# Splitting fp32 operands for one-pass matmuls: ScalarE's copy in place of a mask on VectorE

## The reference, cut to what matters

```
# 1  linear attention, 16 heads of 8
q = elu(x @ Wq + bq) + 1 ;  k = elu(x @ Wk + bk) + 1 ;  k = k / sqrt(sum_head(k*k) + 1e-6)
a = (q @ (k^T @ v) per head) @ Wo + bo
x = layernorm(x + (layernorm(x + a) * gamma + beta))
# 2  cross attention over 64 context rows, 16 heads of 64
p = softmax((x @ Wq2) @ (ctx @ Wk2)^T / 8) ;  x = layernorm(x + (p @ (ctx @ Wv2)) @ Wo2)
# 3  gated MLP, 352 wide; inputs and weights rounded in blocks of 16 to a 4-bit grid times max/6
x = layernorm(x + quant(silu(quant(x) @ quant(Wg)^T) * (quant(x) @ quant(Wu)^T)) @ quant(Wd)^T)
```

## Time and profile before

| | |
|---|---|
| median of 3 runs | 372.44 us (372.42 to 372.96) |
| span of the profiled execution | 371.1 us |
| PE busy | 349.7 us (94%) |
| DVE busy | 308.7 us (83%) |
| POOL busy | 269.0 us (73%) |
| ACT busy | 253.6 us (68%) |
| DMA queues | a few per cent of the span each |

### The profile page before, as it was taken

The page is one execution under the profiler, slowest core; times in us unless marked ns, Lnnn a source line. Parts: engine busy times, 40 slices in busy tenths (PEclk is TensorE's granted clock), DMA queues, the critical chain, the costliest instruction groups (busy, mean ns, idle before and its releaser), DMA issues.

```text
span 371.1 us, 7329 instructions
## 1 busy us (share of the span) xinstructions
PE 349.7 (94%) x2147; PEld 267.9 (72%) x2147; DVE 308.7 (83%) x858; ACT 253.6 (68%) x533; POOL 269.0 (73%) x453
## 2 busy tenths in 40 slices
PE   8999989999998999999999999999999999998774
PEld 7788646675775868787678877786767787887653
DVE  3998557567689998869989779979998998999994
ACT  2957766577676677678688767878767666864553
POOL 4404459958988699969689895898988569784535
PEclk9999999999999999999999999999999999999999
DMA  8900100001000001000000000100000000000010
GB/s 248 305 2 16 30 1 16 14 16 29 15 17 14 17 0 44 28 18 16 29 14 17 14 1 17 31 0 0 17 15 2 15 2 1 15 16 14 3 30 28
DMA packets 13586, 10.44 MB, mean 28 GB/s; under 512 B 971, under 2 KB 12396, under 8 KB 13548
## 3 DMA queue, kind: packets, MB, share of 16 engines
q1 hardware_dynamic: 12540, 7.89, 7.1%
q10 hardware_dynamic: 1008, 2.10, 1.7%
HBM read 7.88 MB, written 2.10 MB: 27 GB/s over the span
## 4 chain that ended last, share of the span: by engine, by line
PE 70%; DVE 9%; POOL 8%; issue 6%; ACT 4%; DMA 1%; SPq 0%; POOLq 0%; DVEq 0%
PE A L2892 13%; PE S L2862 12%; PE TP L2852 7%; PE F L2916 6%; PE TP L2880 6%; PE A L2936 5%; PE S L2871 3%; PE A L2813 2%; PE TP L2791 2%; POOL pe L440 2%; PE F L2791 2%; PE S L2791 2%; PE TP L2925 2%; PE A L2826 2%; PE A L2821 1%
## 5 line engine op out<-in xcount | busy, mean ns | idle before, releaser
L440 POOL TENSOR_TENSOR pe<-pe,srec 128x1024 f32<-128x1024 f32 x32 | 60.9, 1904 | 9.2 <-DVE srec L1860 8.9
L2862 PE MATMUL S<-M,x1T 128*128 128x512 f32 x128 | 60.7, 597 | 1.5 <-ACT pe L1076 1.4
L2892 PEld LDWEIGHTS A<-wvoT,wqkT 128*128 128x128 f32 x480 | 56.4, 192 | 3.1 <-issue 1.8
L2892 PE MATMUL A<-wvoT,wqkT 128*128 128x128 f32 x480 | 58.0, 276 | 0.1
L434 POOL TENSOR_TENSOR fold<-pe 128x512 f32<-128x512 f32 x32 | 40.9, 1277 | 14.6 <-ACT pe L1076 14.4
L1843 DVE TENSOR_REDUCE smax<-S 128x16 fp32r<-128x1024 f32 x32 | 38.7, 1211 | 3.3 <-PE S L2862 3.1
L1076 ACT ACTIVATE pe<-S 128x1024 f32<-128x1024 f32 x32 | 32.6, 1019 | 10.6 <-PE S L2871 10.3
L1081 ACT ACTIVATE wqkT<-TP 128x1024 f32<-128x1024 f32 x32 | 32.6, 1018 | 4.3 <-PE TP L2880 4.1
L2862 PEld LDWEIGHTS S<-M,x1T 128*128 128x128 f32 x128 | 22.2, 190 | 18.3 <-issue 15.3
L2916 PE MATMUL F<-w_gu_r,GT 128*128 128x352 f32 x168 | 35.1, 344 | 0.1
L2880 PE MATMUL TP<-ident,pe 128*128 128x128 f32 x256 | 33.5, 274 | 1.6 <-POOL pe L440 0.9
(11 more groups left out here) (247 smaller groups left out, 888.2 us busy)
## 6 DMA issues: line engine op xcount, KB each, us to landing
xT<-in_x_t SPq DMA_DIRECT2D x16, 128.0 KB, 2.2
x_sb<-in_x SPq DMA_DIRECT2D x16, 128.0 KB, 2.2
out<-yf SPq DMA_DIRECT2D x15, 128.0 KB, 1.8
M<-in_fw SPq DMA_DIRECT2D x1, 560.0 KB, 11.0
wqkT<-in_wq_t ACTq DMA_DIRECT2D x2, 256.0 KB, 4.6
wqkT<-in_wk_t ACTq DMA_DIRECT2D x2, 256.0 KB, 6.1
ctx_f<-in_ctx_t ACTq DMA_DIRECT2D x2, 256.0 KB, 7.0
wvoT<-in_wv_t ACTq DMA_DIRECT2D x1, 512.0 KB, 9.4
```

The source lines that it names most:

```text
L440: ge.tensor_tensor(w, w, spread(srec[n % NFO][:, :], HX, R), ALU.mult).then_inc(pn_made, 1)
L2862: last = te.matmul(S[:, half * BANK:half * BANK + BANK], x1T[b % 2][:, t * P:t * P + P], M[:, b // BH, HC * half:HC * half + HC, b % BH * ...
L2892: last = te.matmul(part(A2, t), pT[n % 2][:, j, :], vo[b % 2][:, j, :], start=(j == 0 and b not in SUM_ON_PE), stop=(j == NJ - 1))
```

## The change

The mask goes. ACT copies the source itself into the high half, which is typed fp32r. The low part then subtracts what was written there, read back as fp32. The scratch tile `xf_cut`, the semaphores of the masks and 23 DVE instructions fall away: 2 masks of ctx, 4 of G, 2 of the gate and up weights and 15 of the MLP inputs, one for each of batches 0 to 14. None is added. All that is left stays in its order on every engine; only the operands and the waits of the copies and the subtractions differ.

```diff
@@ POOL
             def context_low(half):
-                pool.wait_ge(c_cut, half + 1)
+                pool.wait_ge(c_high, half + 1)
                 cols = slice(512 * half, 512 * half + 512)
-                ge.tensor_tensor(ctx_r[:, 1, cols], ctx_f[:, cols], high_bits[half], ALU.subtract).then_inc(c_low, 1)
+                ge.tensor_tensor(ctx_r[:, 1, cols], ctx_f[:, cols], ctx_r[:, 0, cols].bitcast(FP32),
+                                 ALU.subtract).then_inc(c_low, 1)
             def gate_up_low(m):
-                pool.wait_ge(gu_cut_made, m + 1)
-                ge.tensor_tensor(w_gu_r[:, 1, m, :], w_gu[:, m, :], gu_cut[m], ALU.subtract).then_inc(gu_low_made, 1)
+                pool.wait_ge(gu_high_made, m + 1)
+                ge.tensor_tensor(w_gu_r[:, 1, m, :], w_gu[:, m, :], w_gu_r[:, 0, m, :].bitcast(FP32),
+                                 ALU.subtract).then_inc(gu_low_made, 1)
@@ ACT
             def context_high(half):
-                act.wait_ge(c_cut, half + 1)
-                sc.activation(ctx_r[:, 0, 512 * half:512 * half + 512], high_bits[half], ACT.Copy).then_inc(c_high, 1)
+                act.wait_ge(ctx_loaded[half], 16)
+                cols = slice(512 * half, 512 * half + 512)
+                sc.activation(ctx_r[:, 0, cols], ctx_f[:, cols], ACT.Copy).then_inc(c_high, 1)
             def g_keep_high(half, par):
-                k = 2 * half + par
-                act.wait_ge(g_cut, k + 1)
-                sc.activation(g_tile(half, par)[0], high_bits[2 + k].rearrange("p (a b) -> p a b", a=4),
+                act.wait_ge(g_made, half + 1)
+                sc.activation(g_tile(half, par)[0], G_BANKS[half][par].rearrange("p (a b) -> p a b", a=4),
                               ACT.Copy).then_inc(g_high, 1)
             def gate_up_high(m):
-                act.wait_ge(gu_cut_made, m + 1)
-                sc.activation(w_gu_r[:, 0, m, :], gu_cut[m], ACT.Copy).then_inc(gu_high_made, 1)
+                act.wait_ge(fwT_kept, m + 1)
+                sc.activation(w_gu_r[:, 0, m, :], w_gu[:, m, :], ACT.Copy).then_inc(gu_high_made, 1)
@@ ACT, keep_xfT(b)
-                    act.wait_ge(xf_cut_made, b + 1)
-                    sc.activation(xf_r[b % 2][:, 0, :], xf_cut[:, :], ACT.Copy).then_inc(xfT_kept, 1)
+                    act.wait_ge(xfT_made, b + 1)
+                    sc.activation(xf_r[b % 2][:, 0, :], A2[:, 0:T * P], ACT.Copy).then_inc(xfT_kept, 1)
@@ DVE
-            def context_cut(half):
...
-            def g_cut_high(half, par):
...
             def g_keep_low(half, par):
                 k = 2 * half + par
-                dve.wait_ge(g_cut, k + 1)
+                dve.wait_ge(g_high, k + 1)
                 ve.tensor_tensor(g_tile(half, par)[1], G_BANKS[half][par].rearrange("p (a b) -> p a b", a=4),
-                                 high_bits[2 + k].rearrange("p (a b) -> p a b", a=4), ALU.subtract).then_inc(g_low, 1)
+                                 g_tile(half, par)[0].bitcast(FP32), ALU.subtract).then_inc(g_low, 1)
-            def gate_up_cut(m):
...
-            def xf_cut_high(b):
-                dve.wait_ge(xfT_made, b + 1)
-                wait_free(dve, xfT_kept, b)
-                ve.tensor_scalar(xf_cut[:, :].bitcast(INT32), A2[:, 0:T * P].bitcast(INT32), HIGH_MASK, None,
-                                 ALU.bitwise_and).then_inc(xf_cut_made, 1)
-
             def xf_keep_low(b):
-                dve.wait_ge(xf_cut_made, b + 1)
-                ve.tensor_tensor(xf_r[b % 2][:, 1, :], A2[:, 0:T * P], xf_cut[:, :], ALU.subtract).then_inc(xf_low_made, 1)
+                dve.wait_ge(xfT_kept, b + 1)
+                ve.tensor_tensor(xf_r[b % 2][:, 1, :], A2[:, 0:T * P], xf_r[b % 2][:, 0, :].bitcast(FP32),
+                                 ALU.subtract).then_inc(xf_low_made, 1)
@@ DVE, the list of steps
             biases()
-            context_cut(0)
-            g_cut_high(0, 0)
-            g_cut_high(0, 1)
             g_keep_low(0, 0)
             k_features(0)
             g_keep_low(0, 1)
             k_sums(0)
-            g_cut_high(1, 0)
-            g_cut_high(1, 1)
             q_features(0)
             g_keep_low(1, 0)
             g_keep_low(1, 1)
             k_guess(0)
-            context_cut(1)
...
```

More of the change, by code:

```diff
@@ L149, in decoder_layer @@
         xam = several("xam", 2, [P, NX])
-        xf_cut = sb("xf_cut", [P, T * P])
         xf_r = [GT[:, k, 0:2 * T, :].rearrange("p (s t) n -> p s (t n)", s=2) for k in range(2)]
@@ L167, in decoder_layer @@
         fw_m, fw_s, fw_r = (hT[1][:, 0, NWB * k:NWB * k + NWB] for k in range(3))
-        gu_cut = [w[:, 1, 0:I] for w in hT]
-        high_bits = [w[:, 512 * k:512 * k + 512] for w in pe_ for k in range(2)]
         A1, A2, S, TP, F = banks("A1", 1), banks("A2", 1), banks("S", 2), banks("TP", 2), banks("F", 2)
@@ L207, in decoder_layer @@
         bias_made = sem("bias_made")
-        c_cut, c_high, c_low = sem("c_cut"), sem("c_high"), sem("c_low")
-        g_made, g_cut, g_high, g_low = sem("g_made"), sem("g_cut"), sem("g_high"), sem("g_low")
+        c_high, c_low = sem("c_high"), sem("c_low")
+        g_made, g_high, g_low = sem("g_made"), sem("g_high"), sem("g_low")
         m_made = sem("m_made")
@@ L234, in decoder_layer @@
         xfT_made, xfT_kept = sem("xfT_made"), sem("xfT_kept")
-        xf_cut_made, xf_low_made = sem("xf_cut_made"), sem("xf_low_made")
-        gu_cut_made, gu_high_made, gu_low_made = sem("gu_cut_made"), sem("gu_high_made"), sem("gu_low_made")
+        xf_low_made = sem("xf_low_made")
+        gu_high_made, gu_low_made = sem("gu_high_made"), sem("gu_low_made")
         gu_made, th_made, hg_made, h_made = sem("gu_made"), sem("th_made"), sem("hg_made"), sem("h_made")
@@ L1715, in biases @@
                                  ALU.subtract).then_inc(bias_made, 1)
-            def context_cut(half):
-                dve.wait_ge(ctx_loaded[half], 16)
-                ve.tensor_scalar(high_bits[half].bitcast(INT32), ctx_f[:, 512 * half:512 * half + 512].bitcast(INT32),
-                                 HIGH_MASK, None, ALU.bitwise_and).then_inc(c_cut, 1)
-            def g_cut_high(half, par):
-                dve.wait_ge(g_made, half + 1)
-                ve.tensor_scalar(high_bits[2 + 2 * half + par].bitcast(INT32), G_BANKS[half][par].bitcast(INT32),
-                                 HIGH_MASK, None, ALU.bitwise_and).then_inc(g_cut, 1)
             def g_keep_low(half, par):
                 k = 2 * half + par
-                dve.wait_ge(g_cut, k + 1)
+                dve.wait_ge(g_high, k + 1)
                 ve.tensor_tensor(g_tile(half, par)[1], G_BANKS[half][par].rearrange("p (a b) -> p a b", a=4),
-                                 high_bits[2 + k].rearrange("p (a b) -> p a b", a=4), ALU.subtract).then_inc(g_low, 1)
+                                 g_tile(half, par)[0].bitcast(FP32), ALU.subtract).then_inc(g_low, 1)
             def m_keep(half, hd):
@@ L1742, in hw_keep @@
                                TP1.rearrange("p (a b) -> p a b", a=4)).then_inc(hw_kept["dve"], 1)
-            def gate_up_cut(m):
-                dve.wait_ge(fwT_kept, m + 1)
-                ve.tensor_scalar(gu_cut[m].bitcast(INT32), w_gu[:, m, :].bitcast(INT32), HIGH_MASK, None,
-                                 ALU.bitwise_and).then_inc(gu_cut_made, 1)
             def weights_max():
@@ L2073, in _ @@
             m_keep(1, 5)
-            gate_up_cut(0)
             keep_kvT(0)
@@ L2077, in _ @@
             m_keep(1, 7)
-            gate_up_cut(1)
             k_sums(2)
@@ L2201, in _ @@
             statistics("post", 4)
-            xf_cut_high(0)
             aggregate("post", 4)
@@ L2229, in _ @@
             statistics("post", 5)
-            xf_cut_high(1)
             xf_keep_low(1)
@@ L2267, in _ @@
             statistics("attn", 6)
-            xf_cut_high(2)
             k_guess(9)
@@ L2318, in _ @@
             q_features(8)
-            xf_cut_high(3)
             keep_kvT(8)
@@ L2329, in _ @@
             statistics("ffn", 2)
-            xf_cut_high(4)
             xf_keep_low(4)
@@ L2385, in _ @@
             attn_residual(9)
-            xf_cut_high(5)
             statistics("attn", 9)
@@ L2434, in _ @@
             statistics("post", 10)
-            xf_cut_high(6)
             xf_keep_low(6)
@@ L2492, in _ @@
             aggregate("attn", 11)
-            xf_cut_high(7)
             xf_keep_low(7)
@@ L2524, in _ @@
             score_max(11, 0)
-            xf_cut_high(8)
             xf_keep_low(8)
@@ L2572, in _ @@
             score_max(12, 1)
-            xf_cut_high(9)
             xf_keep_low(9)
@@ L2585, in _ @@
             score_max(13, 0)
-            xf_cut_high(10)
             xf_keep_low(10)
@@ L2611, in _ @@
             statistics("cross", 12)
-            xf_cut_high(11)
             keep_kvT(15)
@@ L2665, in _ @@
             statistics("cross", 14)
-            xf_cut_high(12)
             aggregate("cross", 14)
@@ L2676, in _ @@
             gate_times(12, 0)
```

(2 more changed lines are left out.)

## The result

| | before | after |
|---|---|---|
| median of 5 runs | 372.69 us | 379.54 us (379.44 to 379.63) |
| ratio | | 1.0182 (95% interval 1.0171 to 1.0193) |
| span of the profiled execution | 371.1 us | 377.9 us |

The profiled execution of after took 379.63 us as a whole, 1.7 us above its span.

The account below looks back on a forecast made before the run. PE was taken as the bound from about 14 us, so only delays reaching PE count: 371.1 us span + 2.3 at the start + 3.1 in the batches + 1.3 around the span = 377.8 us, range 374.0 to 380.3.

Parts of the forecast that it names:

- What bounds the kernel: From about 14 us PE is the bound; DVE time saved gives nothing by itself, only when PE gets its inputs counts.
- The start: G's split waits for ACT's copies, so PE's solid stretch starts at 16.54 us, not 14.26: +2.3 us, not won back.
- Batches 2, 4, 8 and the tail: Later MLP-input subtractions reach PE: +0.4 us, +1.15, +0.6, and +0.65 in the tail (batches 12 and 13).
- Batches 1, 7, 10, 11: Later MLP-input subtractions: +0.3 us in batch 1, nothing in 7 (hidden), 10 and 11 taken as 0.
- What lies around the span: Time of an execution outside the profiled span, taken as 1.3 us and added to the span.
- Only the start costs: Rival: stalls in the batches die out before PE meets them, 374.7 us; chance 0.27.
- The stalls add up: Rival: all 11 later subtractions in the batches reach PE in full, +6.8 us there, 381.5 us; chance 0.12.
- DVE's relief wins: Rival: dropping masks shortens the start by 1.2 us and the batches behind 240 us by 2.6, 368.6 us; chance 0.07.
- Does less than it says: Rival: ACT writes all bits into the high half, leaving the low half zero; time unchanged at 377.8 us; no chance given.
- A lower clock: Rival: PE's new breaks of 0.6 to 1 us at the start lower TensorE's clock; given nothing of its own.

Follow-up runs that it names:

- experiment 5: Changed kernel with ACT's copies of G moved early at the start and its MLP-input copies moved early in eight batches, no masks: 373.03 us, ratio 1.0004.
- experiment 8: Changed kernel with start masks back; in the batches DVE itself copies A2 into the high half and subtracts, ACT's 15 copies removed: 372.92 us, ratio 1.0000.
- experiment 1: Changed kernel with the masks of the context and G put back at the start, MLP inputs still split by ACT's copy: 377.48 us, ratio 1.0122.
- experiment 3: Changed kernel with only ACT's list at the start reordered, so G's copies come earlier: 377.24 us, ratio 1.0118.
- experiment 4: Changed kernel with ACT's MLP-input copy moved ahead by one or two instructions in eight batches, start left as changed: 375.85 us, ratio 1.0088.
- experiment 6: Changed kernel with the DVE mask put back for batches 4 and 11 alone: 377.79 us, ratio 1.0129.
- experiment 2: Changed kernel with the DVE mask put back for all 15 MLP inputs, start still split by ACT's copy: 376.40 us, ratio 1.0089.

## Why the prediction was right, and where it was short

The forecast was 377.8 us, 5.1 us above the 372.69 of before; measured were 379.54, 6.9 above, inside the range.

**What bounds the kernel: right.** Experiments 5 and 8 take 8 us off DVE or 5 off ACT and change nothing.

**The start: right.** Copies at 9.85, 11.86, 14.71 and 15.2 us, the third product at 16.68; +2.3 was said, +2.4 came. Experiments 1 and 3 give it back in two ways. The saying that it is not won back holds: the delay is 2.4 still at 61 us.

**Batches 2, 4, 8 and the tail: right** to 0.15 us each, and experiments 4 and 6 show that the cause is ACT's place in its list. Batch 8 came by the way that I had named. In two places the sum was luck. In batch 4 I had all of the 1.15 reach PE at 173.45; but 0.45 of it is already there at 167.75 (171.36 in the changed kernel), where PE waits to write A2, as in batch 8, a wait that I had not seen. And in the tail I had 0.24 from batch 12 and 0.43 from batch 13; batch 12 gives nothing, and batch 13 gives the 0.5.

**Batches 1, 7, 10, 11: too small.** They came to 2.0 us where 0.3 stood. The step that failed is where I took PE's need to begin. I had it from the chain of waits, in which a group of matmuls starts when the one before has ended; in the timeline the same group starts 0.2 to 0.3 us earlier, and that is when its operands have to be there. Batch 7: the subtraction ended at 242.88 by my sum (242.09, when ACT comes free, and 0.38 and 0.41), which I held against 242.93 in the chain; the timeline has PE's `gate_up(7,0)` at 242.72. Batch 10 is the same: 288.07, the end of its subtraction before, and 0.4 make 288.47, ahead of 288.51 in the chain and behind 288.35 in the timeline. Both views of the kernel before, the chain (start, us, what) first:

```profile
119.98 0.96 PE F L2916 x6
...
242.93 1.01 PE F L2916 x6
...
288.51 1.78 PE A L2892 x16
```

```profile
119.68 1.27 PE L2916 MATMUL F<-w_gu_r,GT 128*128 128x352 f32 x6
...
242.72 1.05 PE L2916 MATMUL F<-w_gu_r,GT 128*128 128x352 f32 x5
...
288.35 1.95 PE L2892 MATMUL A<-wvoT,wqkT 128*128 128x128 f32 x16
```

In the changed kernel the products of batches 1 and 7 start 0.15 us behind the end of the subtraction (timelines of PE and DVE):

```profile
122.53 1.21 PE L2872 MATMUL F<-w_gu_r,GT 128*128 128x352 f32 x6 [0.17 <-DVE GT L1879]
...
247.26 1.20 PE L2872 MATMUL F<-w_gu_r,GT 128*128 128x352 f32 x6
...
246.69 0.42 DVE L1879 TENSOR_TENSOR GT<-A,GT 128x256 fp32r<-128x256 f32 x1 [1.15 <-ACT GT L1092]
```

So a stall that I called hidden was not hidden. In batch 1 I had 0.3 us come by DVE's later steps at 123.17; it is 0.5, and it comes at the first gate and up product, the upper line, which I had taken as served in time (119.98 against 119.98 in the chain). For batch 8 I happened to use the timeline, and it fits.

For batch 11 there was another error: against 1.5 us I set 0.5 of DVE's waiting and PE's full work beside it, and called the rest 0, "at most 1". The lines of batch 11 above show DVE without a break between the subtraction and the score maximum: what was left came through in full, 0.6 at the maximum, and 0.4 more at 307 us, where PE waits for ACT, which had waited for DVE.

**What lies around the span** was taken as 1.3 us, from the median of other executions. In the runs with a span of their own it is 1.7 to 1.8 (377.9 and 379.63). 0.4 of the 1.7 us between forecast and measurement is that; the batches are the rest.

**The rivals.** "Only the start costs": no, experiment 1 keeps 4.7 us. "The stalls add up": two thirds of it; the steps behind the start sum to 4.4 us, where all late subtractions in full would be 6.8. "DVE's relief wins": no, and experiment 5 gives it every chance. "Does less than it says": it would not change the time by its own terms, and no run tests it; whether ACT's write cuts or rounds was not measured. "A lower clock": not in the changed kernel, but see below. ACT's copy took 0.378 us from PSUM to SBUF against 0.41 from SBUF to SBUF, so the source counts. What the Trainium skill ("ScalarE: Activation LUTs", Step-by-step: what each stage is for) says of the destination, no run here shows, since it was SBUF in both.

## What to carry to other kernels

When a step goes from "both read one producer" to "one after the other over two engines", its price is not its duration but where it stands in the second engine's list: look at what is queued ahead of it at each place, and move it there before judging the change. Work taken off an engine is worth nothing where the bounding engine doesn't wait for it: DVE was busy for 83% of the time here, and 8 us less of it won nothing in experiment 5. And hold an arrival against the start in the timeline, not against the chain's, before calling a stall hidden; where the margin is below the 0.2 to 0.3 us by which the two views differ here, count it as paid.

## What the runs showed of the hardware that I had not expected

**In some executions the clock falls behind the breaks at the start.** I had given a lower TensorE clock nothing. In the profiled execution of experiment 2 PE's breaks at the start were 1.3 and 1.0 us, and the granted clock fell behind them. Windows of its trace (columns as in the earlier trace rows; the clock is the number behind POOL's):

```profile
9.00:12.00 3.00, 1.87 (x21) 1.32 (x19) 0.91 (x2) 1.24 (x3) 0.00 (x0) 1.00 1.03 329
12.00:15.00 3.00, 1.88 (x6) 1.24 (x7) 1.51 (x4) 2.00 (x5) 2.50 (x2) 0.87 1.09 385
15.00:18.00 3.00, 3.00 (x11) 2.47 (x9) 1.69 (x4) 1.80 (x4) 0.00 (x0) 0.56 0.78 245
```

and of the changed kernel, same columns:

```profile
9.00:12.00 3.00, 1.78 (x19) 1.27 (x18) 1.02 (x2) 1.70 (x5) 0.96 (x1) 1.00 1.06 370
12.00:15.00 3.00, 2.04 (x10) 1.52 (x9) 1.41 (x3) 2.32 (x6) 2.52 (x2) 1.00 1.09 384
15.00:18.00 3.00, 2.31 (x11) 1.65 (x11) 2.08 (x5) 1.71 (x5) 0.00 (x0) 1.00 0.77 241
```

0.56 is the lower level, 1.2 GHz, for most of the 3 us, and the six matmuls of the first two products took 2.62 us in place of 1.66:

```profile
12.16 0.70 PE L2810 MATMUL A<-xT,w_attn 128*128 128x256 f32 x2 [1.29 <-DVE fk L1774]
13.82 2.62 PE L2780 MATMUL F<-ctx_r,GT 128*128 128x512 f32 x6 [0.96 <-DVE GT L1725]
```

That fall is not all of it. This execution was 0.6 us late before those breaks. PE's 26 warm-up matmuls (on `fold`, ahead of G) took 5.92 us in it and 5.02 in the changed kernel, and G's first product starts at 7.30 and not 6.67. In the changed kernel they start 0.21 us apart and the last seven 0.11 apart; in experiment 2 they are 0.21 apart to the last. The record of the clock begins only at 5.4 us in the one and at 7.4 in the other, and half the pace is what the lower level would give; so this too looks like the clock, which here came up later. Timelines of PE, experiment 2 and then the changed kernel:

```profile
1.45 5.92 PE L2969 MATMUL A<-fold 128*128 128x128 f32 x26 [1.45 <-POOL fold L380]
...
1.45 5.02 PE L2936 MATMUL A<-fold 128*128 128x128 f32 x26 [1.45 <-POOL fold L377]
```

And the third product of experiment 2:

```profile
17.82 1.73 PE L2780 MATMUL TP<-ctx_r,GT 128*128 128x512 f32 x6
```

PE's product at 13.82 stands against 13.22 in the changed kernel, 0.6 later, and the third at 17.82 against 16.68, 1.1 later. The fall added the 0.5 between the two.

It does not happen each time. In experiment 2 three of four runs have a mean clock of 0.992 or 0.993 and take 376.3 to 376.6 us, the fourth has 0.997 and takes 375.31. In experiment 4, with the same start, two runs at 0.997 took 375.35 and two at 0.992 and 0.993 took 376.3 and 376.7. So such an execution is about 1 us longer, and in the one that was traced about half of that is the fall at 14 us. All five runs of the changed kernel have 0.998 or 0.999, so none of its 6.9 us is the clock. What decides stays open. The one trace with the fall has a first break of 1.3 us, those of the changed kernel and of experiment 4 without it 0.65 and 0.4, and a second of 0.96 in all three; no run here shows that the breaks are the cause.
